# GpSimd takes over three small additions from VectorE: the constant on the variances, twice, and the running counts per expert

## The reference

```python
x = x + attention(layernorm(x), ctx_1024, mask, Wq, Wk, Wv, Wo)
x = x + moe(layernorm(x), gate_w, wi_gate, wi_up, wo)

# layernorm: (x - mean) / sqrt(var + 1e-5)
# moe, for each of the two choices k:
router_probs = softmax(x_flat @ gate_w.T)
top_k_probs, top_k_idx = top_k(router_probs, 2); top_k_probs /= sum
onehot = (eid[:, None] == experts[None, :])
pos    = (cumsum(onehot, axis=0) - 1)[token, eid]     # rank of the token in its expert
valid  = pos < capacity                                # capacity = 640
disp[eid, pos] = x_flat where valid
out   += top_k_probs[:, k] * (silu(disp @ wi_gate.T) * (disp @ wi_up.T)) @ wo.T
```

## Time and profile before

| | before |
|---|---|
| median of three runs | 383.05 us |
| profiled execution | 382.68 us |
| its span, first to last instruction | 380.7 us |
| mean granted TensorE clock | 0.977 |
| TensorE busy | 345.0 us (91%) |
| VectorE busy | 254.6 us (67%) |
| ScalarE busy | 193.7 us (51%) |
| GpSimd busy | 229.1 us (60%) |
| chain that ended last, by engine | TensorE 64%, VectorE 20%, GpSimd 4%, DMA 3%, ScalarE 2% |

### The profile page before, as it was taken

The page is one execution under the profiler, slowest core; times in us unless marked ns, Lnnn a source line. Parts: engine busy times, 40 slices in busy tenths (PEclk is TensorE's granted clock), DMA queues, the critical chain, the costliest instruction groups (busy, mean ns, idle before and its releaser), DMA issues.

```text
span 380.7 us, 9057 instructions
## 1 busy us (share of the span) xinstructions
PE 345.0 (91%) x3017; PEld 302.5 (79%) x3017; DVE 254.6 (67%) x981; ACT 193.7 (51%) x443; POOL 229.1 (60%) x195
## 2 busy tenths in 40 slices
PE   5889879898999997399999999999999999999970
PEld 1566667677877864288999999999999999999970
DVE  4999999999999997524455565645546455465440
ACT  3577777787878875224333444444434343443320
POOL 6383636575666567740663775755748748378663
PEclk9999999999999999689999999999999999999996
DMA  5898402222323121124237345363463643734232
GB/s 180 245 339 272 140 9 56 77 50 68 84 63 108 46 71 58 58 72 114 22 29 177 28 80 126 36 161 42 39 167 34 130 71 34 176 28 37 25 32 21
DMA packets 41158, 34.33 MB, mean 90 GB/s; under 512 B 8336, under 2 KB 37520, under 8 KB 40976
## 3 DMA queue, kind: packets, MB, share of 16 engines
q1 hardware_dynamic: 26592, 23.67, 21.4%
q0 software_dynamic: 13568, 9.58, 18.4%
q10 hardware_dynamic: 960, 0.60, 0.5%
HBM read 21.12 MB, written 17.73 MB: 102 GB/s over the span
## 4 chain that ended last, share of the span: by engine, by line
PE 64%; DVE 20%; issue 4%; POOL 4%; DMA 3%; ACT 2%; SPq 1%; POOLq 1%; DVEq 0%; ACTq 0%
PE bank L915 18%; PE bank L672 10%; PE bank L674 9%; PE bank L673 9%; DVE mneg L1021 5%; PE bank L775 5%; POOL slots L437 3%; PE bank L743 3%; PE bank L766 2%; DVE xn L1002 2%; DVE stats L988 2%; PE bank L906 2%; DVE rall L1071 2%; DMA maskr<-in_mask 1%; POOL out L471 1%
## 5 line engine op out<-in xcount | busy, mean ns | idle before, releaser
L471 POOL DMA_INDIRECT out<-ys,idx x80 | 125.4, 1568 | 82.2 <-DVE ys L1301 29.6
L1328 DVE TENSOR_TENSOR h<-sg,bank 128x256 f32<-128x256 f32 x160 | 66.0, 418 | 86.5 <-ACT sg L657 79.3
L657 ACT ACTIVATE sg<-bank 128x256 f32<-128x256 f32 x160 | 61.6, 385 | 107.2 <-PE bank L674 106.4
L672 PE MATMUL bank<-ex_hi,w_hi 128*128 128x256 f32 x320 | 95.5, 298 | 1.0
L674 PE MATMUL bank<-ex_lo,w_hi 128*128 128x256 f32 x320 | 89.1, 278 | 0.0
L673 PE MATMUL bank<-ex_hi,w_lo 128*128 128x256 f32 x320 | 89.0, 278 | 0.0
L437 POOL DMA_INDIRECT slots<-rall,slot x64 | 62.9, 983 | 34.0 <-DVE slot L1177 20.6
L915 PE MATMUL bank<-w_raw,h 128*128 128x128 f32 x640 | 78.0, 275 | 0.8 <-DVE h L1328 0.8
L915 PEld LDWEIGHTS bank<-w_raw,h 128*128 128x128 f32 x640 | 74.9, 192 | 1.0 <-DVE h L1328 1.0
L672 PEld LDWEIGHTS bank<-ex_hi,w_hi 128*128 128x128 f32 x320 | 60.3, 188 | 4.3 <-issue 2.5
L673 PEld LDWEIGHTS bank<-ex_hi,w_lo 128*128 128x128 f32 x320 | 60.4, 189 | 0.0
(11 more groups left out here) (122 smaller groups left out, 535.9 us busy)
## 6 DMA issues: line engine op xcount, KB each, us to landing
slots<-in_empty SPq DMA_DIRECT2D x8, 660.0 KB, 11.0
xl<-slots SPq DMA_DIRECT2D x7, 660.0 KB, 7.1
w_raw<-in_wgu SPq DMA_DIRECT2D x8, 512.0 KB, 3.8
w_raw<-in_wdn SPq DMA_DIRECT2D x8, 256.0 KB, 4.3
out<-X SPq DMA_DIRECT2D x16, 128.0 KB, 1.9
X<-in_x SPq DMA_DIRECT2D x3, 512.0 KB, 5.3
out<-ys,idx POOLq DMA_INDIRECT x80, 3.3
slots<-rall,slot POOLq DMA_INDIRECT x64
```

The source lines that it names most:

```text
L471: nc.gpsimd.indirect_dma_start(out=out[:, :], out_offset=bass.IndirectOffsetOnAxis(ap=IDX[v][:, j:j + 1], axis=0), in_=YS[c][:, t, :], in_ ...
L657: nc.scalar.activation(SG[m % 2][:], GATE_PS[m % 2][:, 0:2 * P], ACT.Silu).then_inc(sg_ready, 1)
L672: nc.tensor.matmul(ps, hi, m_hi, start=True, stop=False)
L1328: nc.vector.tensor_tensor(H[n % 2][:, f, :], SG[m % 2][:], UP_PS[m % 2][:, 0:2 * P], ALU.mult).then_inc(h_ready, 1)
```

## The change

GpSimd adds the constant 1e-5 to the variances itself, in front of each power, after waiting for VectorE's moments; VectorE's two additions (L995 and L1065) are gone. GpSimd also keeps SEEN: it waits until TensorE's ranks of the block are there, and adds the one-hot forms of the block's two tiles, one after the other with a wait between; VectorE's reduction over the two tiles (L1118) and its addition (L1146) are gone, and so is the tile ADDED. In GpSimd's step the two additions stand behind the first scatter (which belongs to the block before) and ahead of the scatters of the new block. VectorE's `one_hot` waits for the counts of two blocks before, since GpSimd reads the buffer that it writes.

```diff
--- before.py
+++ after.py
@@ -178,7 +178,6 @@
         WHICH = [s1(f"which{v}", [P, RT, 8], U32) for v in range(2)]
         OH = [s1(f"oh{v}", [P, RT, TOPK, E], BF16) for v in range(2)]
         SEEN = s1("seen", [P, TOPK * E], BF16)
-        ADDED = [s1(f"added{v}", [P, TOPK * E]) for v in range(2)]
         DELTA = [s1(f"delta{v}", [P, RT]) for v in range(2)]
         EXPD = [s1(f"expd{v}", [P, RT]) for v in range(2)]
         DEN = [s1(f"den{v}", [P, RT]) for v in range(2)]
@@ -235,7 +234,7 @@
         ln2_step, ve2_ready, rstd2_ready, rn_ready = sem("ln2_step"), sem("ve2_ready"), sem("rstd2_ready"), sem("rn_ready")
         tx2_full, x2t_ready, lg_full, logit_ready = sem("tx2_full"), sem("x2t_ready"), sem("lg_full"), sem("logit_ready")
         best_ready, which_ready, limit_ready, rden_ready = sem("best_ready"), sem("which_ready"), sem("limit_ready"), sem("rden_ready")
-        recip_ready, added_ready, place_ready, past_ready, seen_ready = sem("recip_ready"), sem("added_ready"), sem("place_ready"), sem("past_ready"), sem("seen_ready")
+        recip_ready, count_step, place_ready, past_ready, seen_ready = sem("recip_ready"), sem("count_step"), sem("place_ready"), sem("past_ready"), sem("seen_ready")
         oh_ready, rk_full, delta_ready, expd_ready = sem("oh_ready"), sem("rk_full"), sem("delta_ready"), sem("expd_ready")
         rk_used, slot_ready = sem("rk_used"), sem("slot_ready")
         sent = [sem(f"sent{v}") for v in range(2)]
@@ -395,6 +394,8 @@
                 nc.gpsimd.memset(V2[:, 4 * n:4 * n + 4], 0.0).then_inc(v2_clear, 1)
 
             def inverse_deviation(k):
+                pool.wait_ge(mv_ready, k + 1)
+                nc.gpsimd.tensor_scalar(VE[:, 4 * k:4 * k + 4], MV[:, 4 * k:4 * k + 4, 1], EPS, None, ALU.add).then_inc(ve_ready, 1)
                 pool.wait_ge(ve_ready, k + 1)
                 nc.gpsimd.tensor_tensor(RSTD[:, 4 * k:4 * k + 4], VE[:, 4 * k:4 * k + 4], HALF[:, 0:4], ALU.pow).then_inc(rstd_ready, 1)
 
@@ -408,6 +409,8 @@
 
             def inverse_deviation2(i):
                 u = i % 2
+                pool.wait_ge(ln2_step, 2 * i + 2)
+                nc.gpsimd.tensor_scalar(VE2[u][:], MV2[u][:, :, 1], EPS, None, ALU.add).then_inc(ve2_ready, 1)
                 pool.wait_ge(ve2_ready, i + 1)
                 nc.gpsimd.tensor_tensor(RSTD2[u][:], VE2[u][:], HALF[:, 0:2], ALU.pow).then_inc(rstd2_ready, 1)
 
@@ -438,6 +441,15 @@
                     out=slots[:, :], out_offset=bass.IndirectOffsetOnAxis(ap=SLOT[:, tile, k:k + 1], axis=0),
                     in_=RALL[:, tile, :], in_offset=None).then_inc(sent[k], 16)
 
+            def seen(m):
+
+                pool.wait_ge(rk_full, m + 1)
+                wait(pool, seen_ready, m)
+                oh = OH[m % 2][:].rearrange("p t k e -> p t (k e)")
+                nc.gpsimd.tensor_tensor(SEEN[:], SEEN[:], oh[:, 0], ALU.add).then_inc(count_step, 1)
+                pool.wait_ge(count_step, m + 1)
+                nc.gpsimd.tensor_tensor(SEEN[:], SEEN[:], oh[:, 1], ALU.add).then_inc(seen_ready, 1)
+
             def step(i):
                 if i + 2 < KBUF:
                     spread_keys(i + 2)
@@ -452,7 +464,12 @@
                     pool.wait_ge(tables, 2)
                     nc.gpsimd.tensor_copy(RALL[:, :, D + 2], C[:, C_TOKEN:C_TOKEN + TILES]).then_inc(tables, 1)
                 first = sum(n for at, n in SENDS.items() if at < i)
-                for n in range(first, first + SENDS.get(i, 0)):
+                late = 1 if i > 3 and i in SENDS else 0
+                for n in range(first, first + late):
+                    send(n)
+                if i in ROUTED:
+                    seen(ROUTED[i])
+                for n in range(first + late, first + SENDS.get(i, 0)):
                     send(n)
 
             over_steps(step)
@@ -991,8 +1008,6 @@
                 for t in tiles:
                     ins = nc.vector.bn_aggr(MV[:, t, :], STATS[:, t, :])
                 ins.then_inc(mv_ready, 1)
-                dve.wait_ge(mv_ready, k + 1)
-                nc.vector.tensor_scalar(VE[:, 4 * k:4 * k + 4], MV[:, 4 * k:4 * k + 4, 1], EPS, None, ALU.add).then_inc(ve_ready, 1)
 
             def norm(b):
 
@@ -1059,11 +1074,6 @@
                     ins = nc.vector.bn_aggr(MV2[b % 2][:, t, :], STATS2[b % 2][:, t, :])
                 ins.then_inc(ln2_step, 1)
 
-            def variance2(b):
-
-                dve.wait_ge(ln2_step, 2 * b + 2)
-                nc.vector.tensor_scalar(VE2[b % 2][:], MV2[b % 2][:, :, 1], EPS, None, ALU.add).then_inc(ve2_ready, 1)
-
             def norm2(b):
 
                 dve.wait_ge(rstd2_ready, b + 1)
@@ -1101,6 +1111,7 @@
 
                 first, tiles, v = tiles_of(m)
                 dve.wait_ge(which_ready, 2 * m + 2)
+                wait(dve, seen_ready, m - 1)
                 order = C[:, C_ORDER:C_BASE].unsqueeze(1).to_broadcast([P, tiles * TOPK, E]).rearrange("p (t k) e -> p t k e", k=TOPK)
                 nc.vector.tensor_tensor(OH[v][:, 0:tiles], order, WHICH[v][:, 0:tiles, 0:TOPK].unsqueeze(3).to_broadcast([P, tiles, TOPK, E]),
                                         ALU.is_equal).then_inc(oh_ready, 1)
@@ -1110,12 +1121,6 @@
                 first, tiles, v = tiles_of(m)
                 dve.wait_ge(best_ready, 2 * m + 2)
                 nc.vector.tensor_tensor(DELTA[v][:, 0:tiles], BEST[v][:, 0:tiles, 1], BEST[v][:, 0:tiles, 0], ALU.subtract).then_inc(delta_ready, 1)
-
-            def added(m):
-
-                first, tiles, v = tiles_of(m)
-                dve.wait_ge(oh_ready, m + 1)
-                nc.vector.tensor_reduce(ADDED[v][:], OH[v][:, 0:tiles].rearrange("p t k e -> p (k e) t"), AX.X, ALU.add).then_inc(added_ready, 1)
 
             def own_ranks(m):
 
@@ -1139,11 +1144,6 @@
                 with nc.allow_low_precision(reason="one whole number and zeros are added"):
                     nc.vector.tensor_reduce(SLOT[:, first:first + tiles], R3[v][:, 0:tiles].rearrange("p t (k e) -> p t k e", k=TOPK), AX.X, ALU.add
                                             ).then_inc(place_ready, 1)
-
-            def seen(m):
-
-                dve.wait_ge(added_ready, m + 1)
-                nc.vector.tensor_tensor(SEEN[:], SEEN[:], ADDED[m % 2][:], ALU.add).then_inc(seen_ready, 1)
 
             def past(m):
 
@@ -1229,11 +1229,8 @@
                     moments2(i - 2)
                 if m is not None:
                     one_hot(m)
-                if there(i - 2):
-                    variance2(i - 2)
                 if m is not None:
                     difference(m)
-                    added(m)
                 if there(i + 3):
                     norm(i + 3)
                 if m is not None:
@@ -1262,7 +1259,6 @@
                 if there(i + 1):
                     row_max(i + 1, 0)
                 if m is not None:
-                    seen(m)
                     weight2(m)
                     final(m)
                 if i in MOMENTS:
```

## The result

Slower: 388.78 us (median of 3 runs, 386.72 to 389.66) against 383.05. The ratio is 1.0146, with an interval of 1.0116 to 1.0177. The forecast was 384.2 with a range up to 386.8, so the sign was right and the size was not. The profiled execution took 388.78 us (span 387.0), 6.3 us of span more than before.

The account below looks back on a forecast made before the run. Taken as bounds: VectorE to 88 us, TensorE from 88 to 139, GpSimd's scatters from 152 to 167. Terms -0.74 + 0.60 + 0.23 + 1.04 = +1.13 us gave 384.2 us from the median 383.05, range 382.2 to 386.8.

Parts of the forecast that it names:

- steps 2 to 4: Early steps, bound by VectorE: -0.57 us for three moment groups in steps 0 to 2, -0.37 in step 3.
- (b): VectorE in each step: compare to difference 0.12 us shorter without the variance add, difference to normalization 0.10 without the reduction.
- the prices on GpSimd: Each small add on GpSimd: 0.15 us for a variance add, 0.17 for a count add, plus a handover of 0.08.
- a pair gives about 0: Steps 4 to 7 as two pairs: second normalization 0.28 us later, then -0.08 and -0.19 come back.
- the port rival: Variance add waits behind both first normalizations (0.5 us) on shared ports: 387.7 us; chance 0.10 together with dear arithmetic.
- the regime of equal steps: Steps 8 to 14: TensorE's step (7.26 us) and GpSimd's loop (7.25) equal, so no loss; only VectorE's step end 0.20 late.
- Ring equal to TensorE's step: Loop of slots, three scatters, power, second normalization, slots: 7.25 us after the change, against TensorE's step of 7.26.
- The dearer scatter (0.08): In each step the scatter behind the moved count adds takes 0.08 us more, as scatters behind arithmetic do.
- The dear-arithmetic rival: Adds cost 0.25 us each plus 0.08 per handover, GpSimd's loop 7.35 us: 386.3 us; chance 0.10 together with port collisions.
- Steps 15 to 17: GpSimd's loop sets steps 15 and 16: +0.60 us for two rounds, then +0.23 for the last variance add.
- The last scatters: End of part one, GpSimd without waits: two pairs of count adds of 0.37 + 0.15 us, +1.04.
- the in-between rival: Adds at 0.12 us and no dearer scatters behind the counts: -1.53 at 88 us, 382.5 us in all; chance 0.27.

Follow-up runs that it names:

- no_last_count: Kernel after without the count additions of block 15, which nobody reads: 397.99 us, ratio 0.9739 to the kernel before on the same chip.
- add_twice: Kernel after with GpSimd's variance add done twice, one after the other with a wait between: 402.01 us, ratio 0.9915 to the kernel before.
- the kernel after again: The changed kernel, unaltered, run once more on another set of chips: 397.74 us, ratio 0.9773 to the kernel before there.
- before_no_keys: Kernel before without SyncE's copies of the keys for blocks 6 to 15 (wrong keys used there): 410.07 us, ratio 1.001.
- variances_only: Kernel before with only the variance adds moved to GpSimd, counts left on VectorE: 401.58 us, ratio 0.9826.
- before_two_late: Kernel before with one scatter of each step moved behind the next step's power, so two wait there: 403.71 us, ratio 0.9925.

## Why the prediction was right or wrong

**Right: steps 2 to 4.** Second normalization of step 4, after less before: -0.72 (forecast -0.94). VectorE's aggregates, compare, difference and first normalization of that step start at 59.02, 59.16, 59.24 and 59.31 in the kernel after: the 0.12 and 0.10 of (b) are gone as worked out. The gain is 0.22 short.

**The term that failed first: the prices on GpSimd.** Assumed were 0.15 to 0.17 for an add; in the kernel after the sixteen variance adds of two columns lie between 0.22 and 0.35, and the count adds took 0.23 and 0.22, with two of 0.48 and 0.36 beside work of VectorE (153.48 and 166.95). The nearest row, the cast of 0.19, was the better guide, and I went below it with a per-column rate taken from powers. The dear side of the stated range (0.25 each) is what came.

**Steps 4 to 7, "a pair gives about 0": wrong.** Measured +0.47 and +0.45 for the two pairs: the difference goes -0.72, 0.00, -0.25, +0.46, +0.20 from step 4 to step 8. The working holds with other sizes: 0.07 and 0.08 more for the two adds, 0.15 for the power of 0.88, 0.03 each for the second power and the scatter; together 0.34 to 0.36. The aggregates began 0.74 earlier (59.02 for 59.76), so the working put the late scatter at 62.45 - 0.74, and at 62.05 it was 0.34 later. That power is the port rival in small. The Trainium skill, "SBUF — State Buffer", section Who interferes with whom, says that a VectorE instruction in a two-port mode and GpSimd's exclude each other for a whole instruction. The trace agrees in part. The normalization of 0.60 is two instructions of 0.34; the power began 0.07 into the second and took 0.15 more, and the adds of steps 10 to 12 began 0.02 to 0.03 into it and took 0.10 more, neither the full 0.34. The adds of steps 4, 6 and 8 began 0.02 into the first and took 0.22. So the price hangs on the start, and the sixteen powers of the kernel before, none of which began inside the second instruction, could not show it.

**The third pair was missed.** Step 8 still has a second power (L400 at 93.39), so step 9 pays like steps 5 and 7: +0.72 from step 8 to step 9. I let the regime of equal steps begin at 8. It begins at 10.

**Ring equal to TensorE's step: wrong by up to 0.15.** In steps 10 to 12, where the variance add begins inside a first normalization on VectorE, it takes 0.34 to 0.35 (0.24 to 0.25 in steps 13 to 15, which have none): add and handover cost 0.43 for the 0.23 assumed. The dearer scatter (0.08) did not come inside the ring. 4.30 + 0.43 = 4.73, with 2.67 from the normalization to the first scatter (111.14 - 108.47): 7.40, and the measured step is 7.41. With the shorter add it is 7.30, and the steps from 12 to 15 measure 7.31, 7.40 and 7.31. From step 9 to 14 the difference grows from 0.92 to 1.46. The dear-arithmetic rival (ring 7.35, 386.3 us) had this right, at a low chance.

**Steps 15 to 17.** Forecast +0.83 with the variance add of the last step, measured +1.79 (1.46 to 3.25). Of this 1.1 fall in the step from 15 to 16, where TensorE ran at the low clock behind its stand of 1.03 us.

**The last scatters.** Two pairs of counts were to cost 1.04; from the late scatter to the last it is 1.53. The first pair costs 0.43 (1.84 for 1.41), below the 0.52 assumed; the second 1.04, half of it (0.52) the pair itself, as no_last_count shows, half a scatter of 1.47 that began inside VectorE's split. The forecast had moved the scatters by a sum of prices and not asked beside what they would then start. The collision that the port rival looked for at the variance adds came here, at 0.5 us.

**Not in the sum at all: the clock behind new stands.** From the last scatter to the end the kernel after takes 1.5 us longer (215.4 for 213.9 us) although nothing of the edit lies there. The rows at 178 to 182 us, granted 0.57, hold about 1.7 us of lost clock (4 x 0.43). The same fall came in add_twice behind the same stand, and not in the kernel after again. Two cases do not prove that the stand is the cause. I had read the earlier trace rows with its 0.66 at the end of part one and not asked what a later last scatter does to a filler of fixed length. The sum put this at nothing without a reason.

The misses by stretch, from the second normalizations and the last scatter: 0.2 up to step 4, 0.7 up to step 8, 1.3 up to step 14, 1.0 up to step 17, 0.5 in the last scatters, 1.5 behind them. Together 5.2 us; the forecast of 1.1 plus 5.2 is the 6.3 us of span. For the recorded pair the prices are read from its traces. No run repeated them there, and on the other chips the ring is not what sets the step; add_twice confirms that it has slack at 8.4 us. One slip in the working changes nothing: the in-between rival has -1.53 at 88 us, but its own terms give -0.94 - 2 x 0.26 = -1.46, so 382.6 us and not 382.5.

## What to carry to other kernels

Before moving small work to another engine, write down that engine's ring (who waits for its last result, and how soon it is asked again), price each small instruction at no less than the shortest one of any kind seen there plus a handover, and see whether the ring stays below the step. A filler or a stand next to a moved event belongs in the sum: here new stands of 1.03 and 1.37 us were followed by a lower clock that took 1.1 and 1.5 us more. Ask also beside which long instruction of VectorE a moved GpSimd instruction will start: beginning 0.6 us into one cost a scatter 0.5 us. And where engines stand for results that are ready, look at what GpSimd's scatters overlap before looking at the engines that stand.

## What the runs showed of the hardware

- The same kernel took 383 us in the recorded runs and 406 to 410 us in all later ones, on four chips; the change cost 1.5% in the first and gained 2.3% on one of the four. Up to 60 us the traces agree within 0.6 us. That the chip is the difference is likely and not shown.
- On those chips the logarithm's hand-over from TensorE, when it falls due while GpSimd issues a scatter, comes in most steps 0.7 to 1.2 us after the scatter's end, or 0.3 to 0.7 after the end of the next one if that follows within 1 us; in a few it comes 1.3 to 2.2 behind. With no scatter in the steps it never came late. The link is not strict: in before_no_keys a scatter ran 0.8 us past one due time (118.67) and the logarithm came at once, and in variances_only one came 1.0 late (due 105.54) though the scatter in front had ended 0.4 before. What in the chip does it, and why the recorded pair doesn't show it, stays open.
- Hand-overs to VectorE are held as well: in before_two_late its correction of the outputs, L1039, stood 0.67 us for products that had long ended.
- GpSimd's small adds cost nearly the same for 2, 4 and 16 columns (0.22 to 0.25 us), but an add of two columns took 0.34 to 0.35 when it began inside the second instruction of VectorE's first normalization, and a power there 0.88 instead of 0.72.
- A scatter that begins inside VectorE's 128x1024 subtraction (1.2 us) ends 0.83 to 0.84 us behind the end of that instruction, 1.47 to 1.89 us long; one that begins within 0.02 us of its start takes 0.96.
